# The first microseconds of a decoder layer: order of the masks, loads and first products

## What is computed

```python
q = (q @ fq1_w.T + fq1_b) * (q @ fq2_w.T + fq2_b)      # q, k, v = x @ w.T by heads
k = (k @ fk1_w.T + fk1_b) * (k @ fk2_w.T + fk2_b)
o = causal(q k^T) v                                     # inter and intra chunk parts
o = o * rsqrt(mean(o * o) + EPS) * norm_w ;  attn = o @ wo.T
x = layernorm(x + attn)
x = layernorm(x + xattn(x, k, fside_S2_0, ctx_2048, ctx_2048))
x = layernorm(x + ffn(x, gate, up, down))               # weights = LUT[code] * scale
```

## Time and profile before

| | us |
|---|---|
| median of 3 runs | 567.82 |
| lowest and highest run | 565.97, 568.54 |
| profiled execution, its time | 566.98 |
| profiled execution, its span (first to last instruction) | 565.2 |
| mean granted TensorE clock (share of full) | 0.993 |

### The profile page before, as it was taken

One profiled execution on the slowest core, in us unless ns is written; L12 is line 12 of the kernel. 1 busy time (PEld: TensorE's weight loads), 2 busy tenths in 40 slices (PEclk: granted clock), 3 DMA queues, 4 the chain that ended last, 5 costly groups with the idle time before them and its releaser, 6 DMA issues.

```text
span 565.2 us, 8876 instructions
## 1 busy us (share of the span) xinstructions
PE 536.5 (95%) x3385; PEld 437.7 (77%) x3385; DVE 374.6 (66%) x782; ACT 148.1 (26%) x259; POOL 124.6 (22%) x195
## 2 busy tenths in 40 slices
PE   5999988989989999999999999999999999799993
PEld 5766766766778888876788888776888888688883
DVE  4899788876768566985355586976454777733334
ACT  3432300152333111242242112141332102233230
POOL 2100068220001446030002445120004570200001
PEclk9999899999999999999999999999999999999998
DMA  6522332130110110014000111022001210000001
GB/s 172 161 74 79 87 108 89 38 111 2 38 57 28 39 57 30 0 39 150 1 1 28 48 47 29 2 72 79 1 0 48 65 39 1 31 7 1 1 1 38
DMA packets 25259, 26.83 MB, mean 47 GB/s; under 512 B 2816, under 2 KB 22784, under 8 KB 25216
## 3 DMA queue, kind: packets, MB, share of 16 engines
q1 hardware_dynamic: 14208, 15.73, 9.7%
q10 hardware_dynamic: 10576, 8.95, 5.2%
q0 software_dynamic: 432, 1.57, 0.8%
HBM read 24.15 MB, written 2.10 MB: 46 GB/s over the span
## 4 chain that ended last, share of the span: by engine, by line
PE 82%; DVE 8%; DMA 4%; issue 3%; POOL 2%; ACT 1%; ACTq 0%; POOLq 0%; SPq 0%; DVEq 0%
PE bank L992 16%; PE bank L994 15%; PE bank L993 15%; PE front_bank L1111 5%; PE front_bank L1114 4%; PE front_bank L1112 4%; PE front_bank L1053 4%; PE front_bank L1040 3%; PE bank L987 3%; PE front_bank L992 2%; PE front_bank L993 2%; PE front_bank L994 2%; PE front_bank L1085 2%; DMA wo_sb<-in_woT 1%; PE front_bank L1064 1%
## 5 line engine op out<-in xcount | busy, mean ns | idle before, releaser
L992 PE MATMUL bank<-x2T_lo,ffn_hi 128*128 128x512 f32 x256 | 110.4, 431 | 3.7 <-DVE inter L935 2.1
L935 DVE TENSOR_TENSOR inter<-bank,inter 128x512 f32<-128x512 f32 x64 | 44.2, 690 | 89.2 <-PE bank L994 88.9
L994 PE MATMUL bank<-x2T_hi,ffn_hi 128*128 128x512 f32 x256 | 101.4, 396 | 0.0
L993 PE MATMUL bank<-x2T_hi,ffn_lo 128*128 128x512 f32 x256 | 101.0, 395 | 0.0
L462 POOL TENSOR_TENSOR qbd<-qT_sb,ctxT_sb 128x256 f32<-128x256 f32 x128 | 79.0, 640 | 70.7 <-PE front_bank L1114 57.0
L412 POOL TENSOR_TENSOR ve<-ve,minus_half 128x2 f32<-128x2 f32 x24 | 17.5, 745 | 298.8 <-DVE ve L755 231.8
L617 ACT ACTIVATE inter_hi<-inter 128x512 fp32r<-128x512 f32 x64 | 40.4, 632 | 143.8 <-DVE inter L935 143.8
L992 PE MATMUL bank<-ffn_lo,inter_hi 128*128 128x256 f32 x256 | 76.8, 300 | 1.1 <-DVE inter_lo L929 1.1
L611 ACT ACTIVATE inter<-bank 128x512 f32<-128x512 f32 x64 | 38.2, 597 | 140.5 <-PE bank L994 140.5
L994 PE MATMUL bank<-ffn_hi,inter_hi 128*128 128x256 f32 x256 | 72.0, 281 | 0.0
L993 PE MATMUL bank<-ffn_hi,inter_lo 128*128 128x256 f32 x256 | 72.0, 281 | 0.0
(11 more groups left out here) (118 smaller groups left out, 794.4 us busy)
## 6 DMA issues: line engine op xcount, KB each, us to landing
toep_sb<-in_toep ACTq DMA_DIRECT2D x64, 128.0 KB, 2.1
xT_sb<-in_xT SPq DMA_DIRECT2D x4, 512.0 KB, 5.6
ctxT_sb<-in_ctxT SPq DMA_DIRECT2D x4, 512.0 KB, 4.7
x_sb<-in_x SPq DMA_DIRECT2D x4, 512.0 KB, 5.5
ctx_sb<-in_ctx SPq DMA_DIRECT2D x4, 512.0 KB, 6.8
out<-ctxT_sb POOLq DMA_DIRECT2D x3, 512.0 KB, 3.4
raw_w<-in_gate_p SPq DMA_DIRECT2D x8, 128.0 KB
raw_s<-in_gate_s SPq DMA_DIRECT2D x8, 128.0 KB
```

The costliest lines, as they stand in the source:

```text
L935: nc.vector.tensor_tensor(inter[:, n % 2, :], up_ps[:, :], inter[:, n % 2, :], ALU.mult).then_inc(inter_ready, 1)
L992: nc.tensor.matmul(ps, w_hi, x_lo, start=start, stop=False, skip_group_check=True)
L993: nc.tensor.matmul(ps, w_lo, x_hi, start=False, stop=False, skip_group_check=True)
L994: return nc.tensor.matmul(ps, w_hi, x_hi, start=False, stop=stop, skip_group_check=True)
```

## The change

GpSimd fills a new tile of ones first, head_one second, and v_sb only after all masks; DVE waits for the first finished mask alone. PE multiplies the ones eight times into a bank that nobody reads at that point, and waits for wq and wk separately. SP waits for xT's landing before it fetches; wv goes from ACT's queue to SP's, between fetch 0 and fetch 1; wo goes out before fetch 3, ctxT before fetch 4, x and ctx before fetch 6. The multiply of wo moves from the opening into `rms` of group 0; the bias op and the skip_mat op move later in DVE's order. PE's waits for wo and for the eight constants are split and moved to their first use.

```diff
--- before.py
+++ after.py
@@ -83,6 +83,7 @@
         b_small = sb("b_small", [P, 6])
         skip_sb = sb("skip_sb", [P, 1])
         minus_half = sb("minus_half", [P, 1])
+        ones = sb("ones", [P, P])
 
         with ExitStack() as early:
             def sbe(name, shape, dt=F32):
@@ -146,8 +147,8 @@
         def sems(*names):
             return [sem(n) for n in names]
 
-        ld_fold, ld_wo, ld_factors, ld_small, ld_xT, ld_x, ld_ctxT, ld_ctx, stored = sems(
-            "ld_fold", "ld_wo", "ld_factors", "ld_small", "ld_xT", "ld_x", "ld_ctxT", "ld_ctx", "stored")
+        ld_wq, ld_wk, ld_wv, ld_wo, ld_factors, ld_small, ld_xT, ld_x, ld_ctxT, ld_ctx, stored = sems(
+            "ld_wq", "ld_wk", "ld_wv", "ld_wo", "ld_factors", "ld_small", "ld_xT", "ld_x", "ld_ctxT", "ld_ctx", "stored")
         ld_w = sems("ld_w_even", "ld_w_odd")
         ld_toep = sems(*[f"ld_toep{i}" for i in range(NTOEP)])
 
@@ -175,8 +176,8 @@
         x1_ready, x2_ready, res_ready = ln_ready
         spread_ready = sems("spread_even_ready", "spread_odd_ready")
 
-        filled, const_ready, pool_mask, kv_ready, prod_ready = sems(
-            "filled", "const_ready", "pool_mask", "kv_ready", "prod_ready")
+        ones_ready, filled, const_ready, pool_mask, kv_ready, prod_ready = sems(
+            "ones_ready", "filled", "const_ready", "pool_mask", "kv_ready", "prod_ready")
 
         last_mm, last_stored = sems("last_mm", "last_stored")
         rstd_ready = sems("rstd_ready1", "rstd_ready2", "rstd_ready3")
@@ -337,18 +338,25 @@
                     load_xT(g, tok)
 
 
+                load_ctxT(g, tok)
+                load_rows(g, seq)
+
+            def load_ctxT(g, tok):
+
                 if isinstance(g, int):
                     sp.wait_ge(*((z_ready, 16 * g) if g else (fold_mm, 4)))
                 else:
                     count(sp, stored, 16, g, -16)
                 sp.dma_start(ctxT_sb[:], ctxT_v[:, :, bass.ds(tok, T)]).then_inc(ld_ctxT, 16)
 
+            def load_rows(g, seq):
+
                 count(sp, x2_ready, NB, g, 0)
                 sp.dma_start(x_sb[:], x_v[:, bass.ds(seq, NB), :]).then_inc(ld_x, 16)
                 sp.dma_start(ctx_sb[:], ctx_v[:, bass.ds(seq, NB), :]).then_inc(ld_ctx, 16)
 
-            sp.dma_start(raw_wq, wq.rearrange("(k p) n -> p k n", p=P)).then_inc(ld_fold, 16)
-            sp.dma_start(raw_wk, wk.rearrange("(k p) n -> p k n", p=P)).then_inc(ld_fold, 16)
+            sp.dma_start(raw_wq, wq.rearrange("(k p) n -> p k n", p=P)).then_inc(ld_wq, 16)
+            sp.dma_start(raw_wk, wk.rearrange("(k p) n -> p k n", p=P)).then_inc(ld_wk, 16)
 
             load_xT(0, 0)
 
@@ -360,10 +368,17 @@
                 src = scales[:, c * QC:(c + 1) * QC].unsqueeze(1).broadcast_to([HT, P // HT, QC])
                 sp.dma_start(raw_s[:, u % 2, :], src).then_inc(ld_w[u % 2], 16)
 
+            sp.wait_ge(ld_xT, 16)
             fetch(0)
+            sp.dma_start(wv_sb[:], wvT.rearrange("(k p) n -> p k n", p=P)).then_inc(ld_wv, 16)
             fetch(1)
-            load(0)
             for u in range(2, len(units)):
+                if u == 3:
+                    sp.dma_start(wo_sb[:], woT.rearrange("(k p) n -> p k n", p=P)).then_inc(ld_wo, 16)
+                if u == 4:
+                    load_ctxT(0, 0)
+                if u == 6:
+                    load_rows(0, 0)
                 if u == UNITS_FIRST:
                     load(1)
                 sp.wait_ge(deq_ready, u - 1)
@@ -383,13 +398,13 @@
         @block.gpsimd
         def _(pool):
 
+            nc.gpsimd.memset(ones[:], 1.0).then_inc(ones_ready, 1)
+            nc.gpsimd.memset(head_one[:], 1.0).then_inc(filled, 1)
+            nc.gpsimd.memset(skip_mat[:], 1.0).then_inc(filled, 1)
             nc.gpsimd.memset(ident[:], 0.0).then_inc(filled, 1)
             nc.gpsimd.memset(causal[:], 1.0).then_inc(filled, 1)
-            nc.gpsimd.memset(head_one[:], 1.0).then_inc(filled, 1)
-            nc.gpsimd.memset(skip_mat[:], 1.0).then_inc(filled, 1)
             nc.gpsimd.memset(minus_half[:], -0.5).then_inc(filled, 1)
-            nc.gpsimd.memset(v_sb[:], 0.0).then_inc(filled, 1)
-            pool.wait_ge(filled, 6)
+            pool.wait_ge(filled, 5)
             masks = ((head_one, HT, DK), (skip_mat, CH, CI))
             for tile, n, w in masks:
                 nc.gpsimd.affine_select(out=tile[:], in_=tile[:], compare_op=ALU.is_ge, fill=0.0, base=0,
@@ -402,8 +417,9 @@
                                     base=0, pattern=[[-1, P]], channel_multiplier=1).then_inc(const_ready, 1)
             nc.gpsimd.affine_select(out=causal[:], in_=causal[:], compare_op=ALU.is_ge, fill=0.0,
                                     base=0, pattern=[[1, P]], channel_multiplier=-1).then_inc(const_ready, 1)
-
-            pool.wait_ge(dve_const, 8)
+            nc.gpsimd.memset(v_sb[:], 0.0).then_inc(filled, 1)
+
+            pool.wait_ge(dve_const, 7)
 
             def rstd(g, ln):
 
@@ -493,8 +509,6 @@
             act.dma_start(f_small[:], fT.rearrange("n p e -> p n e")).then_inc(ld_factors, 16)
             act.dma_start(b_small[:, 0:5], bias).then_inc(ld_small, 16)
             act.dma_start(skip_sb[:], skip).then_inc(ld_small, 16)
-            act.dma_start(wv_sb[:], wvT.rearrange("(k p) n -> p k n", p=P)).then_inc(ld_wo, 16)
-            act.dma_start(wo_sb[:], woT.rearrange("(k p) n -> p k n", p=P)).then_inc(ld_wo, 16)
 
             for i in range(4):
                 if i == 2:
@@ -502,7 +516,7 @@
                 act.wait_ge(fold_mm, i + 1)
                 nc.scalar.activation(fold_hi[:, i].rearrange("p k n -> p (k n)"), fb[i][:, :], ACT.Copy)\
                     .then_inc(foldhi_ready, 1)
-            act.wait_ge(ld_wo, 32)
+            act.wait_ge(ld_wv, 16)
             nc.scalar.activation(wv_hi[:], wv_sb[:], ACT.Copy).then_inc(wvhi_ready, 1)
             act.wait_ge(filled, 6)
             act.wait_ge(bd_ready, 1)
@@ -630,24 +644,21 @@
                                             xT_hi[:, kt, :].bitcast(F32), ALU.subtract).then_inc(xlo_ready, 1)
 
             dve.wait_ge(ld_factors, 16)
-            dve.wait_ge(const_ready, 4)
+            dve.wait_ge(const_ready, 1)
 
             for i in range(4):
                 nc.vector.tensor_tensor(f_bd[:, i, :].rearrange("p (h e) -> p h e", e=DK), head_one[:],
                                         f_small[:, i, :].unsqueeze(1).broadcast_to([P, HT, DK]), ALU.mult)\
                     .then_inc(dve_const, 1)
-            dve.wait_ge(ld_small, 32)
             nc.vector.tensor_copy(head_sel[:], head_one[:, :, 0]).then_inc(dve_const, 1)
             nc.vector.tensor_reduce(half_sel[:], head_one[:, :, 0].rearrange("p (r k) -> p k r", k=2), AX.X, ALU.add)\
                 .then_inc(dve_const, 1)
-            nc.vector.tensor_scalar(skip_mat[:], skip_mat[:], skip_sb[:, 0:1], None, ALU.mult).then_inc(dve_const, 1)
-            nc.vector.tensor_scalar(b_small[:, 5:6], b_small[:, 1:2], DK ** -0.5, None, ALU.mult).then_inc(bd_ready, 1)
-            dve.wait_ge(ld_wo, 32)
-
-            nc.vector.tensor_scalar(wo_sb[:], wo_sb[:], b_small[:, 4:5], None, ALU.mult).then_inc(dve_const, 1)
             for i in range(4):
                 if i == 2:
                     split_x(0)
+                    dve.wait_ge(ld_small, 32)
+                    nc.vector.tensor_scalar(b_small[:, 5:6], b_small[:, 1:2], DK ** -0.5, None, ALU.mult)\
+                        .then_inc(bd_ready, 1)
                 dve.wait_ge(foldhi_ready, i + 1)
                 nc.vector.tensor_tensor(fold_lo[:, i].rearrange("p k n -> p (k n)"), fb[i][:, :],
                                         fold_hi[:, i].rearrange("p k n -> p (k n)").bitcast(F32), ALU.subtract)\
@@ -655,7 +666,9 @@
             dve.wait_ge(wvhi_ready, 1)
             nc.vector.tensor_tensor(wv_lo[:], wv_sb[:], wv_hi[:].bitcast(F32), ALU.subtract)\
                 .then_inc(wvlo_ready, 1)
-            dve.wait_ge(dve_const, 8)
+            dve.wait_ge(const_ready, 4)
+            nc.vector.tensor_scalar(skip_mat[:], skip_mat[:], skip_sb[:, 0:1], None, ALU.mult).then_inc(dve_const, 1)
+            dve.wait_ge(dve_const, 7)
 
             def unpack(n):
                 if n < NU:
@@ -708,6 +721,9 @@
                     .then_inc(sm_ready, 1)
 
             def rms(g, _):
+                if isinstance(g, int) and g == 0:
+                    dve.wait_ge(ld_wo, 16)
+                    nc.vector.tensor_scalar(wo_sb[:], wo_sb[:], b_small[:, 4:5], None, ALU.mult).then_inc(dve_const, 1)
                 count(dve, ms_mm, 2, g, 2)
                 if not isinstance(g, int) or g:
                     count(dve, wide_ready, 1, g, 0)
@@ -966,9 +982,13 @@
         @block.tensor
         def _(pe):
 
-            pe.wait_ge(ld_fold, 32)
+            pe.wait_ge(ones_ready, 1)
+            for _ in range(8):
+
+                nc.tensor.matmul(down_ps[1][:, 0:P], ones[:], ones[:], start=True, stop=True, skip_group_check=True)
             for i in range(4):
```

(6 more changed lines are left out.)

## The result

The changed kernel is slower: 568.96 us against 566.32 (medians of 22 runs each), a ratio of 1.0044 with a 95% interval of 1.0031 to 1.0057, or about 2.5 us. 565.9 was forecast, in a range of 563.4 to 568.5. The profiled execution took 568.64, with a span of 566.9 against 565.2.

The account below looks back on a forecast made before the run. TensorE, busy 95% of the span, was taken to bound the kernel, with DVE pacing the opening. Unpack 0 1.6 us earlier plus 0.3 from fetch 2 gave 1.9 us, from the median 567.82 to 565.9 us, range 563.4 to 568.5.

Parts of the forecast that it names:

- What bounds the opening, and the compute side: Opening: DVE sets the pace from 9.6 to 23.5 us; folds start at 4.9, unpack 0 comes 1.6 us earlier.
- Fetch 2: Opening, unpack 2: its fetch no longer queues behind ctxT, x and ctx, taking 4.4 instead of 4.7 us; 0.3 us gained.
- Products of ones: PE's start: eight products, 3.5 us from about 1.1, displace nothing; the clock rises at 6.3, so most folds run fast.
- Loads, the landing of wv: Opening, SP's queue: xT in at about 6.0, wv issued at 7.4 and landed at 11.1, so wv_hi runs 11.1 to 11.7.
- rival A: Opening, ACT's wv_hi: wv lands too late, at 14.1, unpack 0 at 15.6; slower, 568.9 us; chance 0.10.
- early-issue rule: wv's load: issue a transfer early and wait late; by it the held-back wv would set the pace.
- Later loads: Score steps: ctxT after fetch 3, x and ctx after fetch 5 make following fetches 0.3 us late, hidden by DVE's slack.
- 0.85 us of DVE's slack: Score steps: DVE's mask ends at 30.82, PE's keep_busy at 31.67, so DVE can be 0.85 late before PE waits.
- The row taken as nearest: Fetch 2 of the kernel before, 2.8 us after 1.5 MB and late by only 0.3, taken as the lateness for later loads.
- Rival C: Score steps: x and ctx collide with the fetches, costing 0.7 to 1.5 of the 1.9 gained; about 566.9 us; chance 0.10.
- three signs of being wrong: Opening and score steps: wv_hi waits past 12 us, the score steps stretch, or first scores come before 26 us.
- Sum: Whole kernel: 1.6 from unpack 0 plus 0.3 from its second fetch, 1.9 us faster; 565.9 us from the median.

Follow-up runs that it names:

- e3: Changed kernel with all loads issued as in the kernel before, leaving only the compute-side edits; median 565.14 us, ratio 0.9969 to the kernel before.
- e4: Changed kernel without the eight products of ones; median 569.34 us, ratio 1.0042 to the kernel before.
- e6: Changed kernel with wv, wo and first fetches as before, x and ctx before fetch 15, ctxT before fetch 17; 564.99 us, ratio 0.9971 to the kernel before.
- e2: Changed kernel with wv issued right behind xT, ahead of the wait for xT's landing; median 567.10 us, ratio 0.9993 to the kernel before.
- e12: Changed kernel with x and ctx before fetch 15 and without SP's wait for xT; median 565.36 us, ratio 0.9970 to the kernel before.
- e9: The changed kernel itself, unaltered, measured again; median 568.94 us, ratio 1.0028 to the kernel before.
- e11: Changed kernel with x and ctx cut into eight 128 KB loads, one before each of fetches 6 to 13; 566.25 us, ratio 0.9993 to the kernel before.
- e1: Changed kernel with x and ctx issued before fetch 15 instead of fetch 6; median 566.15 us, ratio 0.9996 to the kernel before.
- e8: Kernel before with only x and ctx moved, to before fetch 6 instead of after fetch 1; median 568.77 us, ratio 1.0026 to the kernel before.
- e7: Changed kernel with x alone before fetch 6 and ctx before fetch 9; median 567.54 us, ratio 1.0004 to the kernel before.
- e5: Changed kernel with x and ctx before fetch 15 and wv issued right behind xT; median 565.72 us, ratio 0.9973 to the kernel before.
- e10: Changed kernel with x and ctx issued from ACT's queue in score step 1 instead of by SP before fetch 6; 568.19 us, ratio 1.0017 to the kernel before.

## Why the prediction was wrong

- **What bounds the opening, and the compute side**: right. f_bd began at 4.21 (4.43), folds at 4.64 (4.9), the first projection at 9.39 (9.7), and with the old loads (e3) unpack 0 came 1.7 us earlier (1.6).
- **Fetch 2** (0.3, as it no longer queues behind ctxT, x and ctx): the number came, 0.43 here, but not the reason in full. e3 gained 0.31 with these loads still ahead of it. So e3's 2.0 at both marks meets the forecast sum of 1.9 partly by luck.
- **Products of ones**: the product length fell near 6, as forecast. e4 can't price the earlier folds, since wv is the bound there. Where it isn't, e3 and e6 do: folds done 1.14 us earlier gave unpack 0 0.89 earlier.
- **Loads, the landing of wv** (11.1): mis-sized, by 1.0 us. xT landed at 6.56, not 6.0, and wv took 4.33 after its issue behind fetch 0, not 3.7. Unpack 0 started at 13.72, not 12.6, so the opening gave 0.94 at the first scores. This is the mechanism of rival A, with a third of its lateness (wv at 12.1, against 14.1 there); the early-issue rule of the Trainium skill named there (DMA: Bandwidth & Descriptors, Rules for kernel authors) pointed the right way, as e2 and e12 show.
- **Later loads** ("I take 0.3, hidden by the 0.85 us of DVE's slack"): this step failed, and it turned the sign. It cost 1.95 us of PE's waits, where nothing was expected. Fetch 6 followed x by 1.9 us, not 3, because fetch 5's issue occupies SP for one of these microseconds. Only fetches behind the load were considered, while fetch 5, issued ahead of it, came 1.1 us late for DVE. The slack itself was read rightly (0.81 of 0.85 us).
- **The row taken as nearest** misled, and why stays open. Fetch 2 of the kernel before was issued when 0.7 of the 1.6 MB ahead of it had moved (178 GB/s from 12.0 to 15.94), so some 0.9 MB still lay ahead, nearly as much as the 1 MB ahead of fetch 6. Yet it took 4.7 us and fetch 6 7.7. The DMA engines moved 270 GB/s in the one wait and 193 in the other, where fetch 5 was still under way too; no run separates these.
- **Rival C** had the mechanism but a bound of 1.5 us, so it ended on the faster side; the measured 2.12 lies above it. It named over 2.7 us of lateness as the point that decides; DVE's masks were 2.76 late, and the opening had given only half of the 1.9. Two of the prediction's three signs of being wrong came: wv_hi waited past 12 us, and the score steps stretched.
- **Sum**: 0.94 gained, 2.12 lost, 1.2 us slower at the sums. The ratio says 2.5. The kernel before falls in two groups: 51 of the 114 runs beside the experiments have a mean granted clock of 0.994 or more and a median of 566.3, 35 have 0.990 or less and 567.9. The changed kernel has 6 of 22 in the first (567.8) and 15 in the second (569.7). At like clock it is 1.5 to 1.8 slower; on one chip (e9 and the runs beside it) 1.7 to 1.9. The rest goes with the larger share of its 22 runs at the lower clock. Why the share is larger was not shown, and in e9 the total is only 1.6.

## What to carry to other kernels

A loop that prefetches one buffer ahead and takes as long as its fetch has no room for a large load: here it paid to cut it into pieces smaller than a fetch, one a step (e11), or to put it behind the loop (e1, e6). Price a moved load against the transfers on both sides of its issue, and before holding a load back so that another may land sooner, look for who waits for it: here xT came 0.4 us earlier and wv 3.9 later. And before a difference of 1 us between two traces is given to an edit, look whether it starts behind the edit: here the clock's rise and the time of one fetch moved by that much with the same code.

## What the runs showed of the hardware

A transfer is slowed by one issued behind it, in the same queue. A fetch of 256 KB (codes and scales) that DVE waited for, with no load near, was usable 3.8 to 4.4 us after its issue (fetches 2 and 4 of e6, fetch 4 of e3 and of the kernel before), though once 5.06 (fetch 9 of e2). With 1 MB issued 1.05 us behind it, it took 5.8 to 6.2 (changed kernel, e2, e4, e8, e9), and with 1 MB issued 1.8 to 2.2 us ahead of it 7.5 to 7.9 (the same five). With 512 KB issued 1.05 us behind it took 5.07 (ctx, e7). Fetch 3, with wo ahead and ctxT behind, took under 4.75 in three executions (changed kernel, e1, e7) and 5.4 to 5.9 in seven (e2, e4, e5, e9 to e12), so that e5's 5.63 is no price of ctxT alone; what decides between the two is not known. From ACT's queue, issued at the same moment, the 1 MB made it 6.2 (e10).

With the products of ones from 1.07 us on in all of them, the length of PE's products fell from 421 to 275 ns before 4.6 us in one execution (e9) and at 7.2 in another (e3).

PE's granted clock falls for a stretch well into the kernel too, in some executions and not in others of like code. Near 490 us PE stands 2.12 us for DVE's `inter` in all 14 traces; behind it the clock falls to 0.50 in seven (changed kernel, e2, e3, e5, e6, e8, e9) and stays at 1.00 in seven. The end of the gap and the window of 493 to 498 us, of the changed kernel and then of the kernel before:

```profile
493.07 0.50 PE L1010 MATMUL bank<-x2T_lo,ffn_hi 128*128 128x512 f32 x1 [2.12 <-DVE inter L951]
...
493.00:498.00 5.00, 4.93 (x21) 4.46 (x22) 2.09 (x4) 1.75 (x3) 0.53 (x1) 0.66 0.30 105
```

```profile
492.28 0.51 PE L992 MATMUL bank<-x2T_lo,ffn_hi 128*128 128x512 f32 x1 [2.12 <-DVE inter L935]
...
493.00:498.00 5.00, 5.00 (x29) 4.20 (x28) 2.00 (x3) 1.60 (x3) 0.00 (x0) 1.00 0.30 105
```

The same 18 products that follow the gap take 4.44 us in the changed kernel and 2.98 in the kernel before, so this fall costs 1.46 us. The two groups of the kernel before, 1.5 us apart, are of the size of one such fall, which is more than several of the edits studied here; that this gap alone makes the groups was not shown.
